# Expert weights loaded and split earlier, scatters paced one tile to a slot, and two tiles of the last projection moved into the first expert slots

## The reference

```python
# layer 1
q = layernorm(x); k = v = ctx                       # ctx (2, 128, 512), no projections
energy = einsum('nqhd,nkhd->nhqk', q, k)            # 16 heads of 32
energy = where(mask == 0, -1e20, energy)
attn = softmax(energy / sqrt(512))
x = x + einsum('nhqk,nkhd->nqhd', attn, v).reshape(2, 2048, 512) @ W_out.T
# layer 2
h0 = layernorm(x)
qz = tanh((h0 @ proj_w.T) / 0.3)
logits = -((6 - qz @ anchors.T) * 0.5) / clip(routing_temp, 0.1)
top2, idx = top_k(logits, 2); wt = softmax(top2)    # 6 experts
h = gelu(einsum('btd,edh->bteh', h0, w1))           # w1 (6, 512, 256)
x = x + einsum('bteh,ehd,bte->btd', h, w2, wt)      # w2 (6, 256, 512)
```

## Time and profile before

| | before |
|---|---|
| runs (us) | 741.72, 741.76, 738.56 |
| profiled execution (us) | 737.62, its span 735.9 |
| PE busy | 615.2 us (84%) |
| VectorE busy | 452.1 us (61%) |
| ScalarE busy | 342.3 us (47%) |
| GpSimd busy | 295.0 us (40%) |
| DMA, q1 (issued by SP) | 91.80 MB, 36.5% of 16 engines |
| DMA, q0 (issued by GpSimd) | 33.56 MB, 14.4% |
| attention part | 0 to about 350 us |
| join, to the start of slot 2 | about 350 to 378 us |
| expert part, slots 2 to 79 | 378 to about 680 us |
| combining batch 1 | to 735.9 us |

### The profile page before, as it was taken

The page is one execution under the profiler, slowest core; times in us unless marked ns, Lnnn a source line. Parts: engine busy times, 40 slices in busy tenths (PEclk is TensorE's granted clock), DMA queues, the critical chain, the costliest instruction groups (busy, mean ns, idle before and its releaser), DMA issues.

```text
span 735.9 us, 15131 instructions
## 1 busy us (share of the span) xinstructions
PE 615.2 (84%) x4628; PEld 468.5 (64%) x4629; DVE 452.1 (61%) x968; ACT 342.3 (47%) x646; POOL 295.0 (40%) x434
## 2 busy tenths in 40 slices
PE   5989999999999998877759898979999999996000
PEld 4765565666666654446548787969899888885000
DVE  4857766666776757457854454665455677656465
ACT  4547855666677565756364444323333333331000
POOL 5425756464465657666703022210002223222664
PEclk9779999999999999998869899989999999999555
DMA  5311222222222332338865355545797888886787
GB/s 175 100 30 44 87 87 87 87 87 87 73 77 98 115 116 100 129 118 310 297 263 176 136 176 173 180 170 182 252 301 237 278 266 278 291 281 199 225 250 246
DMA packets 62577, 126.25 MB, mean 172 GB/s; under 512 B 7974, under 2 KB 11046, under 8 KB 62508
## 3 DMA queue, kind: packets, MB, share of 16 engines
q1 hardware_dynamic: 52268, 91.80, 36.5%
q0 software_dynamic: 10240, 33.56, 14.4%
HBM read 69.24 MB, written 56.10 MB: 170 GB/s over the span
## 4 chain that ended last, share of the span: by engine, by line
PE 53%; issue 13%; DVE 11%; DMA 8%; POOL 6%; SPq 4%; ACT 3%; another core or an unknown queue 1%; DVEq 1%; POOLq 0%; ACTq 0%
PE ps L1438 6%; DMA y_d<-ysb 5%; PE ps L1460 4%; PE ps L1596 3%; PE ps L1483 3%; PE ps L1672 3%; PE ps L1485 3%; PE ps L1484 3%; PE ps L1674 3%; PE ps L1673 3%; PE ps L1634 3%; PE ps L1649 3%; PE ps L1650 3%; PE ps L1648 3%; PE ps L1551 2%
## 5 line engine op out<-in xcount | busy, mean ns | idle before, releaser
L767 POOL DMA_INDIRECT yg<-y_d,sidx x64 | 62.9, 983 | 182.6 <-DVE wst L1281 145.9
L1035 DVE TENSOR_REDUCE nmax<-ps 128x4 f32<-128x512 f32 x128 | 82.3, 686 | 38.9 <-PE ps L1438 38.7
L693 POOL DMA_INDIRECT xs_d<-x,place_now x64 | 65.2, 1018 | 100.2 <-DVE place_now L1100 83.8
L870 ACT ACTIVATE prob<-ps 128x512 f32<-128x512 f32 x128 | 66.1, 602 | 77.8 <-PE ps L1463 73.3
L1648 PE MATMUL ps<-w1H,xgH 128*128 x296 | 90.6, 306 | 3.8 <-DVE xgL L1305 2.5
L1650 PE MATMUL ps<-w1L,xgH 128*128 x296 | 84.2, 284 | 2.0 <-issue 2.0
L1649 PE MATMUL ps<-w1H,xgL 128*128 x296 | 84.1, 284 | 1.0 <-issue 1.0
L953 ACT ACTIVATE xgH<-ps 128x512 fp32r<-128x512 f32 x74 | 44.3, 598 | 83.4 <-PE ps L1634 71.0
L1438 PEld LDWEIGHTS ps<-kfT,qT 32*128 32x128 f32 x1024 | 68.0, 198 | 18.1 <-issue 15.1
L1438 PE MATMUL ps<-kfT,qT 32*128 32x128 f32 x1024 | 75.5, 290 | 2.0 <-DVE nmax L1035 1.5
L1318 DVE COPY ysb<-ps 128x512 f32<-128x512 f32 x74 | 51.0, 689 | 34.9 <-PE ps L1674 20.6
(11 more groups left out here) (195 smaller groups left out, 1369.5 us busy)
## 6 DMA issues: line engine op xcount, KB each, us to landing
xg<-xs_d SPq DMA_DIRECT2D x74, 256.0 KB, 4.2
y_d<-ysb SPq DMA_DIRECT2D x74, 256.0 KB
xin<-in_x SPq DMA_DIRECT2D x32, 256.0 KB, 2.8
x<-in_x SPq DMA_DIRECT2D x32, 256.0 KB, 3.6
x_d<-x SPq DMA_DIRECT2D x32, 256.0 KB
x2t<-x_d SPq DMA_DIRECT2D x16, 256.0 KB, 4.2
x2c<-x_d SPq DMA_DIRECT2D x16, 256.0 KB, 4.9
out_x<-x2c SPq DMA_DIRECT2D x16, 256.0 KB
```

Of the source, the lines that this page charges most:

```text
L693: nc.gpsimd.indirect_dma_start(xs_d, bass.IndirectOffsetOnAxis(ap=place_now[:, n % 2, k, t:t + 1], axis=0), x2[:, n % 4, t, :], None).then ...
L767: nc.gpsimd.indirect_dma_start(yg[:, k, z, :], None, y_d[b], bass.IndirectOffsetOnAxis(ap=sidx[:, k, z:z + 1], axis=0))\
L870: nc.scalar.activation(prob[:, v % 2, h, :], ps[:, B_SC + h, :], ACT.Exp, scale=scale).then_inc(exp_done, 1)
L1035: nc.vector.tensor_reduce(nmax[:, n % 2, :, g * hpg + h], ps[:, token_bank(v, h), :].rearrange("p (t k) -> p t k", t=4), axis=AX.X, op=ALU ...
```

## The change

It has four pieces.

1. **Layout.** The attention's tiles are placed so that each lies under weights that are loaded after its last use: `xin`, `qT2`, `xn` under `w1L`; `kfT`, `qT0`, `nmhl`, `kT`, `selT` under `w2L`; `qT1`, `mT`, `prob0`, `prob1` under `w1H`; `ctok` and the division's tiles under `w2H`. `qT` and `prob` become lists of tiles.
2. **Loads and splits.** SP issues the w1 loads in step 34, four w2 loads in step 38, the zero rows of batch 0 in step 41 (on a new count `pad_ready`, given by `places` of block 3), and the last two w2 loads in step 42. ScalarE's twelve `upper` stand as 2, 3 and 3 in steps 42, 43, 44 and 4 behind the loop (before: 2 and 4 in steps 43 and 44, 6 behind). VectorE's `lower` stand as 2 in step 43 and 2 in step 44, each ahead of the step's `residual`, and then two behind each of the four `residual(7, t)`. SP loads the first four `xg` tiles as soon as `project` of block 6 and the tables of batch 0 are done.
3. **Scatters.** Block 4's tiles 1 to 3 wait for `project(7, 0..2)`; those of blocks 5, 6, 7 stand in slots 7 to 10, 15 to 18 and 23 to 26, one tile to a slot, each behind the w1 product of that slot.
4. **Projection.** `project(7, 2)` and `project(7, 3)`, with their residuals, stand behind the turning of expert tiles 0 and 1, in slots 2 and 3.

```diff
@@ layout
-        att_base = cursor[0]
-        qT = sb("qT", [P, 3, kchunks, blk])
+        w1L_base = cursor[0]
+        cursor[0] += unit_bytes
         xin = sb("xin", [P, 4, emb])
+        qT2 = sb("qT2", [P, kchunks, blk])
         xn = sb("xn", [P, 2, emb])
+        w2L_base = cursor[0]
+        kfT = sb("kfT", [P, batches, kchunks, P])
...
@@
+        w_all = [(z, e) for z in range(2) for e in range(EXPERTS)]
+        UPPER_STEP = {S_LAST - 2: w_all[0:2], S_LAST - 1: w_all[2:5], S_LAST: w_all[5:8]}
+        UPPER_LAST = w_all[8:]
+        LOWER_STEP = {S_LAST - 1: w_all[0:2], S_LAST: w_all[2:4]}
+        LOWER_LAST = [w_all[4:6], w_all[6:8], w_all[8:10], w_all[10:12]]
...
+        def late_tile(i, k):
+            j = TPI * i + k - SPAN + 1 if isinstance(i, int) else -1
+            n = nblk - LATE + j // SPAN
+            return (n, j % SPAN) if j >= 0 and j % SPAN < 4 and n < nblk else None
@@ SP
             def attention(s):
+                if s == L_KEY + 4 * (nblk - 2):
+                    sp.wait_ge(xn_done, ntile)
+                    sp.wait_ge(xt1_ready, ntile)
+                    sp.wait_ge(sc_ready, hpg * 4 * (nblk - 2))
+                    for e in range(EXPERTS):
+                        load_w1(e)
+                if s == L_KEY + 4 * (nblk - 1):
+                    sp.wait_ge(mx_ready, hpg * ntile)
+                    sp.wait_ge(sc_ready, hpg * 4 * (nblk - 1))
+                    sp.wait_ge(mt_ready, nblk)
+                    for e in range(4):
+                        load_w2(e)
+                if s == S_END - 1:
+                    fill_up(0)
                 if s == S_END:
                     sp.wait_ge(sc_ready, hpg * ntile)
...
+                    for e in range(4, EXPERTS):
+                        load_w2(e)
...
-            sp.wait_ge(s_zero, 1)
-            fill_up(0)
-            sp.wait_ge(atL_done, ntile)
-            for e in range(EXPERTS):
-                sp.dma_start(w2L[:, e, :, :].bitcast(F32), w2[e, :, :].rearrange("(j p) d -> p j d", p=P))\
-                  .then_inc(wr_in[EXPERTS + e], 16)
-            for t in range(3):
-                store_rows(INSIDE, t)
             scattered_all(0)
             sp.wait_ge(pad_zero[0], 16 * EXPERTS)
-            sp.wait_ge(out_ready, ntile)
+            sp.wait_ge(tab_done, 3)
+            sp.wait_ge(out_ready, 4 * INSIDE)
             row = rows_from(0)
-            for k in range(-L_X):
+            for k in range(TPI):
                 load_rows(row[k], k, k)
-            store_rows(INSIDE, 3)
+            for t in range(4):
+                store_rows(INSIDE, t)
@@ GpSimd
             row_factors(INSIDE - 1)
             for t in range(4):
+                if t > 0:
+                    pool.wait_ge(out_ready, 4 * INSIDE + t)
                 scatter(INSIDE - 3, t)
             row_factors(INSIDE)
-            for n in range(INSIDE - 2, nblk):
-                for t in range(4):
-                    scatter(n, t)
...
+                    z = late_tile(i, k)
+                    if z is not None:
+                        pool.wait_ge(up_ready, TPI * i + k - L_UP + 1)
+                        scatter(*z)
@@ ScalarE
-                if s == S_LAST - 1:
-                    for e in range(2):
-                        upper(0, e)
-                if s == S_LAST:
-                    for e in range(2, EXPERTS):
-                        upper(0, e)
+                for e in UPPER_STEP.get(s, ()):
+                    upper(*e)
...
-            for e in range(EXPERTS):
-                upper(1, e)
+            for e in UPPER_LAST:
+                upper(*e)
@@ VectorE
+                if m == blk_per_batch - 1:
+                    dve.wait_ge(used_done, n + 1)
+                    nc.vector.tensor_copy(tab_pad[:, b, :], used[:, b, blk_per_batch, :]).then_inc(pad_ready, 1)
...
+                for e in LOWER_STEP.get(s, ()):
+                    lower(*e)
                 if i >= 0:
                     residual(i, q)
...
-            lower(0, 0)
-            lower(0, 1)
-            residual(INSIDE, 0)
...
-            for e in range(EXPERTS):
-                lower(1, e)
+            for t in range(2):
+                residual(INSIDE, t)
+                for e in LOWER_LAST[t]:
+                    lower(*e)
...
+                    if isinstance(w, int) and w in (0, 1):
+                        residual(INSIDE, 2 + w)
+                        if w == 1:
+                            moments(INSIDE)
+                        for e in LOWER_LAST[2 + w]:
+                            lower(*e)
@@ PE
-            for t in range(4):
+            for t in range(2):
                 project(INSIDE, t)
-            pe.wait_ge(tab_done, 4)
+            pe.wait_ge(tab_done, 3)
...
                         last.then_inc(xt_ready, 1)
+                    if isinstance(w, int) and w in (0, 1):
+                        project(INSIDE, 2 + w)
```

More of the change, by code:

```diff
@@ L517, in _ @@
             attention_loop(attention)
[L519 to L524, removed]
-                for e in range(EXPERTS):
-                    row = sp.snap(row_regs[e], min_val=0, max_val=batches * rows - P)
-                    sp.dma_start(xs_d[bass.ds(row, P), :], zeros[:]).then_inc(pad_zero[b], 16)
             def scattered_all(b):
@@ L573, in experts @@
                     w, p, n = tl(i, k, L_X, 4)
-                    if live(w, tiles):
+                    if live(w, tiles) and not (isinstance(w, int) and w < TPI):
                         load_rows(row[k], w, p)
@@ L840, in upper @@
                 act.wait_ge(wr_in[EXPERTS * z + e], 16)
+                act.wait_ge(sc_ready, hpg * ntile)
+                act.wait_ge(pv_done, ntile - 1 if z == 0 and e < 5 else ntile)
+                if z == 1 and e >= 2:
+                    act.wait_ge(raw_done, ntile)
+                    act.wait_ge(less_done, ntile)
+                    act.wait_ge(at_done, ntile)
+                    act.wait_ge(atL_done, ntile)
                 nc.scalar.activation(wH[:, e, :, :], wL[:, e, :, :].bitcast(F32), ACT.Copy).then_inc(wH_done, 1)
@@ L1197, in rows_of_tokens, with lower @@
                                         mine, moved[:], ALU.add).then_inc(tab_done, 1)
+            def lower(z, e):
+                wH, wL = (w1H, w1L) if z == 0 else (w2H, w2L)
+                dve.wait_ge(wH_done, EXPERTS * z + e + 1)
+                nc.vector.tensor_tensor(wL[:, e, :, :], wL[:, e, :, :].bitcast(F32), wH[:, e, :, :], ALU.subtract)\
+                  .then_inc(wL_done, 1)
             def attention(s):
@@ L1251, in _ @@
             attention_loop(attention)
-            def lower(z, e):
-                wH, wL = (w1H, w1L) if z == 0 else (w2H, w2L)
-                dve.wait_ge(wH_done, EXPERTS * z + e + 1)
-                nc.vector.tensor_tensor(wL[:, e, :, :], wL[:, e, :, :].bitcast(F32), wH[:, e, :, :], ALU.subtract)\
-                  .then_inc(wL_done, 1)
-            lower(0, 0)
-            lower(0, 1)
-            residual(INSIDE, 0)
-            lower(0, 2)
-            lower(0, 3)
-            residual(INSIDE, 1)
-            lower(0, 4)
-            residual(INSIDE, 2)
-            lower(0, 5)
-            residual(INSIDE, 3)
-            moments(INSIDE)
-            for e in range(EXPERTS):
-                lower(1, e)
+            for t in range(2):
+                residual(INSIDE, t)
+                for e in LOWER_LAST[t]:
+                    lower(*e)
             def stage(c, q):
@@ L1459, in scores_by_key @@
                     r = h * HD
-                    mm(ps[:, B_SC + h, :], kT[r:r + HD, b, g, :], qT[r:r + HD, n % 3, g, :], start=True, stop=False)
+                    mm(ps[:, B_SC + h, :], kT[r:r + HD, b, g, :], qT[n % 3][r:r + HD, g, :], start=True, stop=False)
                 for h in range(hpg):
@@ L1550, in attention @@
                     for h in range(hpg):
-                        last = mm(ps[h * HD:(h + 1) * HD, B_DEN, :], ones[:], prob[:, v % 2, h, :], start=True, stop=True)
+                        last = mm(ps[h * HD:(h + 1) * HD, B_DEN, :], ones[:], prob[v % 2][:, h, :], start=True, stop=True)
                     last.then_inc(sums_ready, 1)
@@ L1595, in attention @@
                         c = g * P + h * HD
[L1596 removed]
+                        last = mm(ps[h * HD:(h + 1) * HD, B_NUM, :], ctok[:, b, c:c + HD], prob[v % 2][:, h, :],
                                   start=True, stop=True)
```

67 lines of the change are left out of this document (39 added, 28 removed).

## The result

Four runs of the changed kernel gave a median of 721.63 us (719.37 to 723.70), beside 740.68 us (738.56 to 741.76) for four of the kernel before. The ratio is 0.9746, 95% interval 0.9706 to 0.9786: 19 us faster. The medians of this document are over all executions, the ratios over those in the fast state alone, and a ratio is an estimate of its own, not the quotient of two medians. The profiled execution took 719.37 us, its span 717.6.

What follows compares the result with a forecast made beforehand. PE bounds nearly everywhere, but idles 11.61 us at the join by queue order and loses 18.4 beside scatter bursts; 737.6 - 8.1 - 14.8 + 1.0 = 715.7, or 719.8 against the median; forecast 718, range 709 to 731.

Steps and rivals of the forecast that it cites:

- likeliest case: Whole kernel: gains at the join and in the expert slots both come, 713 to 723 us, chance 0.56.
- What bounds the kernel: At the join PE idles 11.61 us through a queue order; three long expert slots beside scatter bursts lose 18.4 us.
- each falls at the end of a burst: Expert slots: the three long ones each come as eight scatters of one block end, scatters 1.27 us apart.
- Scatters: Expert slots: pacing recovers 14.8 of 18.4 us, leaving 0.3 in each of twelve slots; bounds 0 and 18.4.
- Loads: Attention steps 34, 38, 41 and 42: the earlier weight loads cost 0 to 1.1 us at each of three places, 1 in all.
- Splits: Steps 43 and 44: four `lower` in VectorE's queue delay `project(7, 0)` by 2.5 us, bounds 0 and 4.7.
- port rule: VectorE with two SBUF inputs and GpSimd reading SBUF exclude each other; up to 1.1 us per step on GpSimd, sum unchanged.
- What is late next: Slots 2 to 5: VectorE's queue delays `xgL` of tile 2; 18.9 us, 6.2 of it new, slot 6 at 382.8.
- The join in all: From the removed w2 wait to slot 6: net gain 8.1 us, bounds 4 and 11.
- Pacing does not help: Expert slots: two scatters a slot still stall; gain 8.1 + 0 to 6, 724 to 733, say 729 us; chance 0.16.
- VectorE takes the join's gain: Slots 2 to 5 slip and steps 43 and 44 cost 4.7; join gain 2, total 724 us; chance 0.11.
- slower case: Dense DMA stretches starve engines of instructions, stopping twelve paced slots and three load places; 756 us, chance 0.05.

Runs made afterwards that it cites:

- both measurements: The unaltered changed kernel measured twice beside the kernel before: 721.6 us against 740.7, ratio 0.9746; then 718.3 against 723.4, ratio 0.9937.
- second trace: The kernel before, unaltered, profiled again on another measurement's chip: 729.4 us in one run, median there 723.4.
- unpaced kernel: The changed kernel with the scatters of blocks 4 to 7 unpaced again, all else kept: 741.6 us beside 744.1, ratio 0.9978.
- pacing alone: The kernel before with only the scatters of blocks 5, 6, 7 paced, one tile to a slot: 725.7 us beside 744.1, ratio 0.9788.
- first trace: The original profile of the kernel before, unaltered, on which the prediction was made: profiled execution 737.62 us.
- two changes of order: The changed kernel with steps 43 and 44's four lowers behind step 44 and block 5's router work ahead of `residual(7, 2)`: 715.3 us, ratio 0.9899 to the kernel before.

## Why the prediction was right, and where it was not

The time, 721.6, lies in the range, 3.6 above the forecast, and the likeliest case held. Of its two gains one was too small and one too large. The forecast is a time, and the changed kernel takes about the same in both measurements (721.6 and 718.3); the gain, which is what was reasoned out, is 19 us in one and about 5 in the other. That the gain came out close to what was reasoned hangs on which measurement it was, and is luck in that.

**What bounds the kernel.** Right for the join: the ScalarE wait for w2 had one cause, and PE's wait behind it went (11.61 to 0.72 us). Right that the long slots belong to the bursts, in the measurements that have them. The step that failed is "each falls at the end of a burst", read as a property of the kernel. In the second trace the same burst costs nothing, so of 19 us only about 5 carry over.

**Scatters.** 14.8 forecast, with 0.3 left in each paced slot; 18.4 in the traces, nothing left. The upper bound was the value. By times 15.8, and 17.2 from the unpaced kernel (0.9978 - 0.9746, from different measurements). The paced load, 512 KB in 3.5 us, is 27% below the burst's, not 30%.

**Loads.** 1.0 forecast, about 0 measured: from step 37 to step 41 the changed kernel and pacing alone, which has no loads there, both take 35.3 us, and steps 34 to 36, with the w1 load, take 0.2 us more. The row at 387 GB/s and PE full was the nearest one, not the one at 510 to 520 us.

**Splits.** 2.5 forecast between bounds 0 and 4.7. From `residual(6, 0)` to `project(7, 0)` it was 349.75 - 325.40 = 24.35 before and 359.65 - 330.29 = 29.36 after, 5.0 more. But 1.5 of that is step 42 with its clock; against pacing alone (25.9) and the second trace (26.0), where the clock fell too, the splits cost 3.4 to 3.5, inside the bounds and 1.0 over the forecast. The excess matches one thing: a pair of lowers beside GpSimd's product took 3.47 instead of 2.35. The port rule was set aside with "my sum stays"; it was worth about 1.1 here, on VectorE's side, where I had looked only at GpSimd's.

**What is late next.** The mechanism was named right, VectorE's queue of slots 2 to 5, with `xgL` of tile 2 behind the last lowers. Its size was not: 6.2 more forecast, and 20.4 - 12.2 = 8.2 from the turning of tile 0 to that of tile 4. Slot 6 started at 391.7, not at 382.8: 4.9 us of that came before step 41, 1.5 in step 42, 1.0 from the splits and some 1.6 behind the start of `project(7, 0)`. I had the router work end at 373.9 and the residual of tile 3 follow; in fact the router work stood behind the idle 2.95 us, and ScalarE's exponentials with `xgH` behind it.

**The join in all.** 8.1 forecast, 5.6 measured where the clock fell in step 42 both before and after (4.1 against the first trace, where it did not). The lower bound, 4, was nearer.

**The sum against one execution.** The profiled execution of the kernel before had kept its clock in three steps: 33 and 37, where every other trace takes 1.6 to 5 us longer, and 42, where all but one take 1.5 longer. Against it the join's gain seems to be -0.8 us; against the second trace it is 5.6, against the pacing-alone kernel 5.1.

**The rivals.** "Pacing does not help" came true where nothing stalls, for another reason than mine. "VectorE takes the join's gain" came half true. The slower case, more stops for instructions in dense stretches, is refuted for the loads (333 GB/s, nothing lost) and for the paced slots. Its mechanism is not borne out by the packets of the queues that the page of the profile calls "instruction". In the second trace of the kernel before they fall inside and beside bursts without any stall. In the two traces that stall, none lands while PE stops in the first burst (405 to 408 in the kernel before, 412 to 415 with unpaced scatters); the next ones come only 4 and 3 us later, and at the later bursts they lie inside the burst again. No row shows that an engine waited for one, and none excludes it for the other stops. What stalls the engines in two of the measurements stays open.

## What to carry to other kernels

When waiting weights are loaded earlier, ask next which engine must prepare them and where its instructions stand in its queue: twelve subtractions of 1.2 us, each pair ahead of something that another engine waits for, gave back a good part of the removed wait, and two changes of order with no work removed shortened the join by 4.7 us in the traces (3.0 by the medians). Measure a part of the kernel between two landmarks of its own, over several traces, before believing a difference of whole executions, and look at the clock between the landmarks too: a clock that fell by chance in three steps hid some 6 us here. One of the three lay inside my own measure. And measure a stall more than once, on more than one chip, before its removal is called the kernel's gain.

## What the runs showed of the hardware

- The same burst of eight indirect scatters (256 KB every 1.27 us) stops ScalarE, VectorE and PE for 4 to 7 us in the traces of two of the measurements and not at all in the trace of a third; the kernel before takes 741 to 744 us in the first two and 723.5 in the third and in a fourth, of which there is no such trace. Up to the stop the DMA share was much the same (0.77 against 0.80).
- GpSimd subtractions of 2.4 us stretch VectorE instructions of 0.2 to 0.3 us on SBUF to 1.9 to 2.3 us, but not the reductions beside them (0.30 and 0.18).
- A PE pause of some 1.5 us in step 37 left the clock at 2.4 GHz in one execution and was followed by the 1.2 GHz level in others of the same code, at a cost of 1.6 to 3.2 us. A pause of 2.1 us in step 42 did the same: clock kept in 2 of 14 traces, 1.5 us lost in the others.
